# A cross-attention's value product and projection: split products of 128 columns for fp32 products of 64

## What is computed

```
x = x + xattn(layernorm(x), ctx)
q, k, v = x @ wq.T, ctx @ wk.T, ctx @ wv.T          # ctx: 16 x 512 x 512
attn = softmax(q @ k.T / 8), masked                 # one head of 512 features
out  = attn @ v                                     # 64 x 512 for each sequence
out  = swapaxes(out, 1, 2).reshape(64, 512)         # features and tokens exchanged
out  = out @ proj_w.T + proj_b
```

## Time and profile before

| | |
|---|---|
| median of 3 runs | 1212.85 us (1212.16 to 1214.77) |
| the profiled execution | 1213.19 us |
| its span | 1211.4 us |
| mean granted clock of TensorE | 0.972 of 2.4 GHz |
| TensorE busy | 91% of the span |
| VectorE, ScalarE, GpSimd busy | 48%, 31%, 16% |
| first cross-attention | from the start to 188.06 us |

### The profile page before, as it was taken

The page is one execution under the profiler, slowest core; times in us unless marked ns, Lnnn a source line. Parts: engine busy times, 40 slices in busy tenths (PEclk is TensorE's granted clock), DMA queues, the critical chain, the costliest instruction groups (busy, mean ns, idle before and its releaser), DMA issues. The chain is left out here.

```text
span 1211.4 us, 17827 instructions
## 1 busy us (share of the span) xinstructions
PE 1101.9 (91%) x6507; PEld 678.1 (56%) x6528; DVE 578.3 (48%) x995; ACT 377.1 (31%) x1012; POOL 193.5 (16%) x187
## 2 busy tenths in 40 slices
PE   7999999999899999999998999956998999994986
PEld 4544457887344444444443655456696868773542
DVE  2233145886732322411112544266848475668766
ACT  1211135666311001210001222244424233246863
POOL 0011001333222310000000112025122121300004
PEclk9999999999999999999998999978999999997999
DMA  9964802001011100000007777740000000007001
GB/s 345 387 233 165 312 1 70 2 1 36 26 35 35 41 2 1 1 0 0 0 1 258 269 278 277 278 173 1 1 1 0 0 0 0 0 0 286 1 1 70
DMA packets 55128, 108.61 MB, mean 90 GB/s; under 512 B 4144, under 2 KB 4528, under 8 KB 55088
## 3 DMA queue, kind: packets, MB, share of 16 engines
q1 hardware_dynamic: 55088, 108.09, 25.1%
HBM read 105.98 MB, written 2.10 MB: 89 GB/s over the span
## 5 line engine op out<-in xcount | busy, mean ns | idle before, releaser
L1705 ACT ACTIVATE f_act<-bank,f_sgn 128x512 f32<-128x512 f32 x64 | 44.0, 687 | 267.8 <-PE bank L1660 262.3
L1660 PE MATMUL bank<-f_a_hi,f_w 128*128 128x512 f16 x512 | 115.7, 379 | 0.0
L1660 PE MATMUL bank<-f_a_lo,f_w 128*128 128x512 f16 x512 | 115.7, 379 | 0.0
L1734 DVE CAST f_b_hi<-f_act 128x512 f32 x32 | 25.5, 796 | 165.6 <-ACT f_act L1705 165.6
L1660 PEld LDWEIGHTS bank<-f_a_lo,f_w 128*128 x512 | 50.1, 98 | 60.4
L1660 PEld LDWEIGHTS bank<-f_a_hi,f_w 128*128 x512 | 50.1, 98 | 60.2
L653 POOL TENSOR_TENSOR x_mv<-x_mv,eps 128x2 f32<-128x2 f32 x9 | 1.7, 192 | 439.2 <-DVE x_mv L534 439.2
L1510 DVE TENSOR_TENSOR s_e<-s_pair,s_tables 128x512 f32<-128x512 f32 x64 | 41.4, 687 | 42.0 <-POOL s_kT L1570 24.8
L373 PE MATMUL bank<-x_cT,x_qT 128*64 128x512 f32 x256 | 60.3, 616 | 0.0
L398 PE MATMUL bank<-x_cN,x_eT 128*64 128x512 f32 x256 | 56.9, 596 | 0.0
L1392 ACT ACTIVATE s_e<-bank,s_nmax 128x64 f32<-128x64 f32 x128 | 38.0, 336 | 50.3 <-DVE s_nmax L1456 50.3
(11 more groups left out here) (315 smaller groups left out, 2263.8 us busy)
## 6 DMA issues: line engine op xcount, KB each, us to landing
x_cT<-in_ctx_cols_dram SPq DMA_DIRECT2D x32, 1024.0 KB, 7.6
x_cN<-in_ctx_rows_dram SPq DMA_DIRECT2D x32, 1024.0 KB, 9.5
f_upper_bits<-in_f_w_dram SPq DMA_DIRECT2D x20, 256.0 KB, 2.7
s_wv_raw<-in_s_wv_dram SPq DMA_DIRECT2D x3, 1024.0 KB, 10.7
f_raw<-in_f_wd_dram SPq DMA_DIRECT2D x1, 2816.0 KB, 17.6
x_qw<-in_x_qw_dram SPq DMA_DIRECT2D x8, 256.0 KB, 4.4
x_kw<-in_x_kw_dram SPq DMA_DIRECT2D x8, 256.0 KB, 4.9
x_vw<-in_x_vw_dram SPq DMA_DIRECT2D x2, 1024.0 KB, 14.6
```

The source lines that it names most:

```text
L1660: mm = pe.matmul(h_bank[s][:, :], weights(2 * i + s, k), part[:, k, cols], start=(n == 0 and k == 0), stop=(n == 1 and k == k_chunks - 1))
L1705: act.activation(act32[s][:, :], h_bank[s][:, :], ACT.Relu, scale=sgn[:, layer % 2:layer % 2 + 1]).then_inc(h_read, 1)
L1734: dve.tensor_copy(hi[:, 2 * i + s, :], act32[s][:, :]).then_inc(hhi_ok, 1)
```

## The change

It works on the first cross-attention alone (`proj is not None`).

- The value product becomes, for each slot, twelve split products of 128 columns (tokens of both sequences) by 512; the projection likewise. The second cross-attention has had the value product in this form.
- ScalarE casts the high parts of both weights, p_hi and v_hi, once, after the first queries' copies and ahead of the first exponential, and waits for both loads before; DVE makes v_lo and p_lo once, in the first turn between the maxima and the reciprocals. The low parts take the place of the loaded weights in memory.
- ScalarE's copy of o, one instruction of 128x512 before, is now four of 64x256, since the output no longer lies where the projection wants it. DVE then makes o_hi (a copy) and o_lo (a difference), and aT_lo before.
- In the last turn the split of the head attention's value weights moves behind aT_lo, o_hi and o_lo on DVE.
- v_hi and p_hi lie where qw and kw lay (hence the wait on `m_done`), and the head attention's wk and wq over slot 0's cT.

```diff
         with ExitStack() as early:
-            vw_sb = core.sbuf(early if proj is None else st, f"{tag}_vw", [P, KC, D])
+            vw_sb = core.sbuf(early, f"{tag}_vw", [P, KC, D])
+            if proj is not None:
+                proj_sb = core.sbuf(early, f"{tag}_proj", [P, KC, D])
+        if proj is not None:
+            v_lo, p_lo = (sb(n, [P, KC, D], F32R) for n in ("v_lo", "p_lo"))
+            v_hi, p_hi = spare_weights
...
-            aT = slot("aT", [P, KC, P])
-            o_sb = slot("o", [P, 2, HALF])
+            aT_hi = slot("aT_hi", [P, KC, P], F32R)
+            aT_lo = slot("aT_lo", [P, KC, P], F32R)
+            o_sb = slot("o", [P, KC, 2, SEQ])
+            o_hi = slot("o_hi", [P, KC, 2 * SEQ], F32R)
+            o_lo = slot("o_lo", [P, KC, 2 * SEQ], F32R)
...
-        cT = slot("cT", [P, 2, KC, CTX])
-        cN = slot("cN", [P, 2, MC, D])
+        cT, cN = context if context is not None else (slot("cT", [P, 2, KC, CTX]), slot("cN", [P, 2, MC, D]))
...
                     for s in range(2):
                         pe.wait_ge(aT_ok, 2 * i + s + 1)
-                        pe.wait_ge(v_in, 16 * n_v)
-                        for b in range(2):
+                        pe.wait_ge(vsplit, 4)
+                        for n, (l, r) in enumerate(((aT_hi[s], v_hi), (aT_hi[s], v_lo), (aT_lo[s], v_hi))):
+                            if n == 2:
+                                pe.wait_ge(alo_ok, 2 * i + s + 1)
                             for k in range(KC):
-                                for h in range(2):
-                                    mm = pe.matmul(bank[O_BANK[s]][SEQ * h:SEQ * (h + 1), b * HALF:(b + 1) * HALF],
-                                                   aT[s][:, k, SEQ * b:SEQ * (b + 1)], vw_sb[:, k, h * HALF:(h + 1) * HALF],
-                                                   start=(k == 0), stop=(k == KC - 1))
+                                mm = pe.matmul(bank[O_BANK[s]][:, :], l[:, k, :], r[:, k, :],
+                                               start=(n == 0 and k == 0), stop=(n == 2 and k == KC - 1))
                         mm.then_inc(o_done, 1)
                     for s in range(2):
-                        pe.wait_ge(o_ok, 2 * i + s + 1)
-                        for k in range(KC):
-                            for b in range(2):
-                                mm = pe.matmul(bank[Y_BANK[s]][SEQ * b:SEQ * (b + 1), :], o_sb[s][:, b, SEQ * k:SEQ * (k + 1)],
-                                               proj_sb[:, k, :], start=(k == 0), stop=(k == KC - 1))
+                        pe.wait_ge(ohi_ok, 2 * i + s + 1)
+                        for n, (l, r) in enumerate(((o_hi[s], p_hi), (o_hi[s], p_lo), (o_lo[s], p_hi))):
+                            if n == 2:
+                                pe.wait_ge(olo_ok, 2 * i + s + 1)
+                            for k in range(KC):
+                                mm = pe.matmul(bank[Y_BANK[s]][:, :], l[:, k, :], r[:, k, :],
+                                               start=(n == 0 and k == 0), stop=(n == 2 and k == KC - 1))
                         mm.then_inc(y_done, 1)
...
             for half in range(2):
                 copy_queries(0, half)
-            if proj is None:
-                act.wait_ge(v_in, 16 * n_v)
-                act.copy(v_hi[:, :, :], vw_sb[:, :, :]).then_inc(vsplit, 1)
+            act.wait_ge(v_in, 16 * n_v)
+            if proj is not None:
+                act.wait_ge(m_done, KC)
+                act.copy(p_hi[:, :, :], proj_sb[:, :, :]).then_inc(vsplit, 1)
+            act.copy(v_hi[:, :, :], vw_sb[:, :, :]).then_inc(vsplit, 1)
             def turn(i, last):
                 for s in range(2):
...
                 for s in range(2):
                     act.wait_ge(aT_done, 2 * i + s + 1)
-                    dst = aT[s] if proj is not None else aT_hi[s]
-                    act.copy(dst[:, :, :], as_chunks(bank[AT_BANK[s]][:, :])).then_inc(aT_ok, 1)
+                    act.copy(aT_hi[s][:, :, :], as_chunks(bank[AT_BANK[s]][:, :])).then_inc(aT_ok, 1)
                     if s == 0 and not last:
                         copy_queries(i + 1, 1)
                 if proj is not None:
                     for s in range(2):
                         act.wait_ge(o_done, 2 * i + s + 1)
-                        act.copy(o_sb[s][:, :, :], bank[O_BANK[s]][:, :].rearrange("p (b n) -> p b n", b=2)).then_inc(o_ok, 1)
+                        for h in range(2):
+                            for b in range(2):
+                                ins = act.copy(o_sb[s][SEQ * h:SEQ * (h + 1), :, b, :],
+                                               bank[O_BANK[s]][SEQ * b:SEQ * (b + 1), h * HALF:(h + 1) * HALF].rearrange("p (k n) -> p k n", k=KC))
+                        ins.then_inc(o_ok, 1)
                         if s == 0 and last and following is not None:
                             following.copy_raw(act, following.wv_hi, following.wv_raw)
...
-                if first and proj is None:
-                    dve.wait_ge(vsplit, 1)
+                if first:
+                    dve.wait_ge(vsplit, 1 if proj is None else 2)
                     dve.tensor_tensor(v_lo[:, :, :], vw_sb[:, :, :], v_hi[:, :, :].bitcast(F32), ALU.subtract).then_inc(vsplit, 1)
+                    if proj is not None:
+                        dve.tensor_tensor(p_lo[:, :, :], proj_sb[:, :, :], p_hi[:, :, :].bitcast(F32), ALU.subtract).then_inc(vsplit, 1)
                 for s in range(2):
                     dve.wait_ge(e_ok, 2 * i + s + 1)
                     dve.reciprocal(small[s][:, 2:3], small[s][:, 1:2]).then_inc(rinv_ok, 1)
...
                     following.split_queries(dve, (2, 3), 3)
-                    following.split_raw(dve, following.wv_lo, following.wv_raw, following.wv_hi, 6)
                 if proj is None:
                     if not last:
                         row_constants(i + 1)
+                for s in range(2):
+                    dve.wait_ge(aT_ok, 2 * i + s + 1)
+                    dve.tensor_tensor(aT_lo[s][:, :, :], as_chunks(bank[AT_BANK[s]][:, :]),
+                                      aT_hi[s][:, :, :].bitcast(F32), ALU.subtract).then_inc(alo_ok, 1)
+                if proj is not None:
                     for s in range(2):
-                        dve.wait_ge(aT_ok, 2 * i + s + 1)
-                        dve.tensor_tensor(aT_lo[s][:, :, :], as_chunks(bank[AT_BANK[s]][:, :]),
-                                          aT_hi[s][:, :, :].bitcast(F32), ALU.subtract).then_inc(alo_ok, 1)
+                        dve.wait_ge(o_ok, 2 * i + s + 1)
+                        rows = o_sb[s][:, :, :, :].rearrange("p k b n -> p k (b n)")
+                        dve.tensor_copy(o_hi[s][:, :, :], rows).then_inc(ohi_ok, 1)
+                        dve.wait_ge(ohi_ok, 2 * i + s + 1)
+                        dve.tensor_tensor(o_lo[s][:, :, :], rows, o_hi[s][:, :, :].bitcast(F32), ALU.subtract).then_inc(olo_ok, 1)
+                if last and following is not None:
+                    following.split_raw(dve, following.wv_lo, following.wv_raw, following.wv_hi, 6)
                 for s in range(2):
                     dve.wait_ge(y_done, 2 * i + s + 1)
                     dve.wait_ge(xb_ok, 2 * i + s + 1)
...
             with ExitStack() as early:
-                qw, kw, wk_raw, wv_raw = (core.sbuf(early, n, [P, KC, D]) for n in ("x0_qw", "x0_kw", "s0_wk_raw", "s0_wv_raw"))
+                cT0 = core.sbuf(early, "x0_cT0", [P, 2, KC, CTX])
+                wk_raw, wv_raw, qw, kw = (core.sbuf(early, n, [P, KC, D]) for n in ("s0_wk_raw", "s0_wv_raw", "x0_qw", "x0_kw"))
             wk_hi, wq_hi, wk_lo, wv_lo = (shared(f"s0_{n}", [P, KC, D], F32R) for n in ("wk_hi", "wq_hi", "wk_lo", "wv_lo"))
+            spare_weights = [shared(f"x0_{n}", [P, KC, D], F32R) for n in ("v_hi", "p_hi")]
...
+            context_stack = ExitStack()
+            context = [[cT0, core.sbuf(context_stack, "x0_cT1", [P, 2, KC, CTX])],
+                       [core.sbuf(context_stack, f"x0_cN{s}", [P, 2, MC, D]) for s in range(2)]]
```

More of the change, by code:

```diff
@@ L163, in cross_attention @@
 def cross_attention(core, block, tag, front, qw_sb, kw_sb, m_hi, m_lo, ctx_rows, ctx_cols, qw, kw, vw, out_bias, scale, mask=None, proj=None,
-                    biases=None, clip=None, ahead=(), x=None, identity=None, following=None):
+                    biases=None, clip=None, ahead=(), x=None, identity=None, following=None, spare_weights=None, context=None):
     nc = core.nc
@@ L189, in cross_attention @@
         if proj is not None:
-            proj_sb = sb("proj", [P, KC, D])
             mask_i = sb("mask_i", [P, MC], I32)
@@ L260, in cross_attention @@
         o_ok = sem("o_ok")
+        ohi_ok = sem("o_hi_ok")
+        olo_ok = sem("o_lo_ok")
         y_done = sem("y_done")
@@ L2171, in program @@
                                      io["x0_qw"], io["x0_kw"], io["x0_vw"], io["x0_pb"], (D // 8) ** -0.5, mask=io["mask"],
```

(4 more changed lines are left out.)

## The result

The changed kernel takes 1216.78 us (median of 20 runs, 1214.07 to 1219.98) against 1212.97 (median of 20, 1211.28 to 1215.86). The ratio is 1.0028, with a 95% interval of 1.0020 to 1.0037: slower by 2.4 to 4.5 us. Forecast: 1215.9, 3.0 more than before, with a range of 1214.6 to 1217.3.

A forecast was written before the change was run, and what follows sets the result against it. TensorE was taken to bound the stage, with small holes. Products gain 11.0 us, the first turn's weight wait loses 13.95 and the clock 0.1: +3.0 on 1212.85 gives 1215.9, range 1214.6 to 1217.3.

The forecast's parts named there:

- The loss: First turn: ScalarE's wait and casts, then DVE's low parts, delay slot 0's attended values from 41.80 to 55.75, 13.95 us lost.
- The gain of a turn: First cross-attention loop: value product and projection take 11.53 us instead of 14.35, 2.82 gained a turn, 8.5 over three.
- The last turn: Last turn before the head attention: 2.5 us gained, with the first key product waiting for DVE's split of value weights.
- The sum: Whole kernel: 13.95 lost plus 0.1 for the clock less 11.0 gained gives +3.0 us, 1215.9.
- The o chain: ScalarE's four o copies and DVE's o_hi, o_lo between the two products: hidden with 0.3 to 0.5 us to spare, costing nothing.
- The clock: First turn after the stall: query projections at half clock, 5 us instead of 2.9; 0.1 taken, 0 to 1.6 kept.
- Rival A: Kinder clock: shifted turns' scores pass their holes at full clock, 2.2 us come back, 1213.7, no difference; chance 0.22.
- Rival B: Harder clock, 1.5 us, or an o chain that shows, 0.4 us a turn: 1217.5 to 1219; chance 0.16.
- Rival C: First turn's wait for weights met early: 2.1 lost, 8.9 faster, 1204; sum negative if landing before 40.7; chance 0.07.
- Rival D: Split products don't pay in the first cross-attention: gain vanishes, loss stays, up to 1226; chance 0.05.

The follow-up runs named there:

- experiment 1: Changed kernel with ScalarE's weight casts after the first turn's exponentials and query copies, and DVE's v_lo and p_lo behind both eT; 1201.18 us, 0.9905; run again 1201.50, 0.9907.
- experiment 4: Changed kernel with SyncE issuing both weight loads ahead of the four context-row loads; 1204.90 us, ratio 0.9942.
- experiment 9: Kernel before, products untouched, plus only the weights' wait and casts ahead of the first exponential and DVE's subtractions ahead of eT; 1228.99 us, ratio 1.0136.
- the tenth: The changed kernel itself, unaltered, measured again on another chip (the second comparison with the kernel before); 1215.15 us, ratio 1.0017.
- experiment 7: Kernel of experiment 1 with DVE doing the next turn's layernorm ahead of the two residual sums; 1195.52 us, ratio 0.9849.
- experiment 8: Kernel of experiment 1 with both weight loads early and the layernorm ahead of the sums; 1195.28 us, ratio 0.9849.
- experiment 12: Kernel of experiment 8 with the head attention's eight small loads issued ahead of its three large ones; 1191.22 us, ratio 0.9820.
- experiment 2: Changed kernel with only DVE's v_lo and p_lo moved behind both eT, ScalarE's casts left in place; 1215.61 us, ratio 1.0022.
- experiment 3: Changed kernel with only ScalarE's wait and casts moved behind the first turn's exponentials and query copies, DVE's splits left; 1214.95 us, ratio 1.0017.

## Why the prediction was right, point by point

- **The loss.** Forecast: casts from 43.73, exponential 47.33, eT done 55.6, attended values 55.75. Measured: 43.88, 47.49, 55.71, 55.81. (The sum reads 49.9 for the end of the xT split and goes on with 49.8; it changes nothing.) Experiments 1, 4 and 9 show that it is this chain. By the start of the attended values it is 14.7 us less without it (41.09), 11.8 less with an early landing (44.01), and 14.2 more with it alone (56.02 for 41.80). That the first scores start at 28.97 here and at 29.71 before changes nothing, since the chain hangs on the load.
- **The gain of a turn.** Forecast 2.82 us, measured 14.35 - 11.71 = 2.64. The step that was off is "of the 5.67 some 0.15 is the change to the next form": both sets of 24 take 5.67 or 5.68 (66.56 to 72.24, 72.24 to 77.91). The hole behind them is 0.1 shorter (4.90 us from scores to transposes instead of 5.00), so the turn gains 2.77 in all. Three turns and the last (2.49, forecast 2.5) give 10.4 for 11.0 in the products.
- **The last turn.** Its 2.49 is the right number partly by luck. The forecast had TensorE ready 11.2 us after its value product began and waiting for DVE's split of the value weights until 11.4. That split ended 11.44 after it (191.16), but TensorE itself was busy until then, since the second 24 products took 5.67 and not 5.5 and it waited 0.1 for o_hi.
- **The sum.** 14.01 lost, less 10.4 in the products and 0.4 in shorter holes and the rest of the turns, is the 3.16 by which the stage ends later. So the forecast's 3.0 is near it also because the products' missing 0.6 was mostly made good elsewhere. The first comparison's 3.4 us (3.8 between its medians) lies above both, the second's 2.1 below.
- **The o chain.** Four pieces 1.50 us (forecast 1.54), rounding copy 0.43 (0.46). TensorE waits for o_hi nowhere in the loop and 0.1 in the last turn, as forecast. The first key product is at 191.22 (forecast 191). The last turn of the kernel after, DVE and then TensorE:

```profile
188.88 2.28 DVE L160 TENSOR_TENSOR s_wv_lo<-s_wv_raw,x_m_hi 128x2048 fp32r<-128x2048 f32 x1
...
188.29 1.20 PE L450 MATMUL bank<-x_p_hi,x_o_hi 128*128 128x512 f32 x4
...
191.22 0.74 PE L807 MATMUL bank<-x_xT_hi,s_wk_hi 128*128 128x256 f32 x4
```

- **The clock.** Forecast half clock for the query projections, hidden behind DVE's low parts but for 0.1; measured 4.19 us for them (50.20 to 54.39) where 5 was taken, and wholly hidden. In another execution of the same kernel (the tenth) all six groups were slow and the attended values began at 56.84. Of these 1.03 us, 0.64 is a later landing (44.52 for 43.88); the rest is the clock, since TensorE began 0.5 us after DVE's eT (55.68 + 0.67) instead of 0.1. So the term can be above nothing, as its range said.
- **Rival A.** Scores behind a hole ran slow (4.5 to 5.4 us instead of 3.65) in 18 of 33 cases in the eleven profiled executions that have the holes (the changed kernel and that of experiment 1 twice), and in none of the 7 cases where experiments 7, 8 and 12 closed them. In the profile after it is two of three, as before (5.28 and 4.51 us for 4.87 and 4.67), so the clock neither gave nor took there. In the tenth, the same kernel, it is one of three: how often it happens differs from one execution to the next. **Rival B** had a harder clock or an o chain that shows, from 1217.5 on. The o chain was hidden, and the median stayed below.
- **Rival C** decided as its step said: with a landing at 32 instead of 43.9 the kernel is about 7 us faster than before (ratio 0.9942, 5.1 to 9.0 us), where the rival had 8.9. Its turning point, 38 to 41, wasn't tried. **Rival D** fell with the 11.71 us of a turn.

## What to carry to other kernels

Work that is done once is not free where it is done: a wait for a load in the middle of a queue holds everything behind it, on that engine and on those that it feeds, so set it by when its result is first used, not by where it is easy to write. Find each engine's last moment for such work from the trace; if two engines share it, move both, since either alone is covered by the other. And when a gain is given back elsewhere, look for the order of queues before giving up the gain.

## What was not expected

The price of an idle stretch depends on what follows it. After some 10 us without work TensorE was granted 0.50 in every trace here that has such a wait (the kernel after and experiments 2, 3, 9 and 10). Where short projections came first this cost nothing in the profiled execution, since DVE was slower still, and 0.4 us in the tenth experiment. In experiment 2, where DVE was done early, the slow projections (50.57 to 55.17) themselves held back the attended values. Where the attended values came first they took 9.76 us for 7.09 (experiment 3), and behind waits of only 1.18 and 2.07 us still 8.78 (experiment 4). The two holes in front of the scores, together 2.0 to 2.3 us, cost 0.9 to 1.7 us more in 18 of the 33 cases.
